# Cross network on one core: transposes and scaled additions interleaved by half-batches, and two neighbouring rows per partition moved by one 4 MB transfer

## The chip, the core and the metric

The kernel runs on one NeuronCore of a Trainium2 chip. The core has a matrix engine (PE, or TensorE), a vector engine (DVE), a scalar engine (ACT), a general engine (POOL), a sequencer that only issues transfers here (SP), and 16 DMA engines that move data between HBM (main memory, "DRAM" in the code) and SBUF (on-chip memory with 128 partitions). The metric is the device time in microseconds of one execution.

## The reference

The input `x0` has 16384 rows of 4096 float32 numbers (256 MiB), and the output has the same shape. Six layers are applied, each with a weight vector and a bias vector of 4096 numbers:

```python
def step(x, wb):
    wi, bi = wb
    xw = jnp.matmul(x, wi)          # one number per row
    x_new = x0 * xw + bi + x
    return (x_new, None)
x, _ = jax.lax.scan(step, inputs, (w, b))
```

After every layer `x` is a multiple of `x0`, one factor per row, plus a vector `c` that is the same for all rows (the sum of the biases so far). So the kernel needs the six dot products of every row of `x0` with the weights, and the constants `cw` (the dot products of `c` with the weights). The factor of a row follows from a recurrence of six steps, factor = factor × (1 + dot) + cw. The output row is factor × x0 + `c_last`.

## The kernel before, in words

The 16384 rows are 128 tiles of 128 rows. A tile is `[128 partitions x 4096]` float32, which is 2 MB (2,097,152 bytes), a row to a partition. Two tiles are a batch (`TB = 2`), so there are 64 batches. SBUF holds eight tiles (`tiles`, slots 0 to 7), which is four batches (`BR = 4`). Slot `s` is loaded for the next time when the store from it has landed.

Every batch goes through these steps:

- SP loads the two tiles, with one transfer each (L141 for the first eight, L145 afterwards). L144 waits for the semaphore `y_stored[s]` of the slot.
- DVE transposes the batch in 32x32 blocks into `blocks`, in four chunks of 128x2048 (L267). Before a chunk it waits until PE is done with that chunk of the batch before (L290).
- PE multiplies the chunks with the weights: 128 matrix products into `dots` (L350).
- ACT copies `dots` four times into `spread` under a mask (L197); PE reduces that to `turned` (L364); ACT adds one and writes `growth` (L202).
- DVE runs the recurrence of six steps, one scan for each tile (L274), and then "finishes" each tile: `tiles = tiles * scale + c_last`, 128x4096, in place (L280).
- ACT stores each finished tile with one transfer (L209).

What sets the order is the program order of each engine, with semaphores between the engines. On DVE it is written in `transpose_and_finish`: four chunks of batch n, then the finish of tile 1 of batch n-1, then the scans of batch n, then the finish of tile 0 of batch n. On ACT the two stores of batch n-1 stand ahead of `make_growth` of batch n, the second of them waiting for the finish of tile 1 of batch n-1. DVE, ACT and SP each run this in a loop over rounds of four batches, with the first round and parts of the last written out.

Ahead of the first batch the weights are loaded into slot 7 four times at different partitions and transposed (L136, L250), and `c_last` is made by PE and ACT (L332, L187). The last batch is finished and stored in eight pieces of 128x1024 (L314, L227), so that the final transfer is small.

The matrix products of a batch start as soon as chunk 0 is transposed, and follow the transposes chunk by chunk.

Of the kernel before, what the change touches and what calls it, by code (L numbers as in the profile page):

```python
# [9 lines left out]
P = 128  # L24
Q = 32
G = P // Q
TB = 2
BR = 4
KM = 2
NCHUNK = 4  # L30
# [4 lines left out]
PIECES = 4  # L35


def cross_network(nc, x, w, b, out):
# [13 lines left out]
    PW = D // PIECES  # L52
    w_rows = w.rearrange("l d a -> l (d a)")
# [3 lines left out]
    with ExitStack() as ctx:  # L57
# [39 lines left out]
        x_landed = [sem(f"x_landed{s}") for s in range(n_slots)]  # L97
        y_stored = [sem(f"y_stored{s}") for s in range(n_slots)]
# [27 lines left out]
        @block.sync  # L126
        def _(sp):
            sp.dma_start(strips_b[:], b_strips).then_inc(strips_b_landed, 16)
            sp.dma_start(strips_w[:], w_strips).then_inc(strips_w_landed, 16)
            sp.dma_start(b_stage, b).then_inc(b_landed, 16)  # L130
            sp.dma_start(tiles[:, 0, :], x[0:P, :]).then_inc(x_landed[0], 16)
# [5 lines left out]
            for s in range(1, n_slots):  # L137
                if s == n_slots - 2:
                    sp.wait_ge(scratch_filled, n_halves)
                    sp.wait_ge(weights_ready, 1)  # L140
                sp.dma_start(tiles[:, s, :], x[s * P:(s + 1) * P, :]).then_inc(x_landed[s], 16)  # L141
# [40 lines left out]
        @block.scalar  # L182
        def _(act):

            for h in range(n_halves):
                act.wait_ge(scratch_filled, h + 1)
                nc.scalar.copy(c_last[:, h * HALF:(h + 1) * HALF], scratch[:]).then_inc(scratch_copied, 1)  # L187
            act.wait_ge(cw_all_ready, 1)
            nc.scalar.copy(cw[:], cw_all[:]).then_inc(cw_ready, 1)

            def make_growth(batch, first=False):
                act.wait_ge(blocks_used, (batch + 1) * NCHUNK)  # L192
                if first:
                    act.wait_ge(group_mask_ready, 1)

                for g in range(G):
                    nc.scalar.activation(spread[:, :, :, g, :], dots[:], ACT.Copy,  # L197
                                         scale=group_mask[:, g:g + 1]).then_inc(dots_spread, 1)
                act.wait_ge(turned_ready, batch + 1)
                if not first:  # L200
# [4 lines left out]
            def store(batch, round_, q):  # L205
                for t in range(TB):
                    s = q * TB + t
                    act.wait_ge(tiles_done, batch * TB + t + 1)
                    act.dma_start(out[bass.ds((round_ * n_slots + s) * P, P), :],  # L209
                                  tiles[:, s, :]).then_inc(y_stored[s], 16)  # L210

            make_growth(0, first=True)
            for q in range(1, BR):
                store(q - 1, 0, q - 1)
                make_growth(q)
            with act.Fori(1, n_rounds) as r:
                store(r * BR - 1, r - 1, BR - 1)
                make_growth(r * BR)
                for q in range(1, BR):
                    store(r * BR + q - 1, r, q - 1)  # L220
                    make_growth(r * BR + q)

            for n in range(TB * PIECES):
                s = n_slots - TB + n // PIECES
                at = slice(n % PIECES * PW, (n % PIECES + 1) * PW)
                act.wait_ge(tiles_done, n_tiles - TB + n + 1)
                act.dma_start(out[(n_tiles - n_slots + s) * P:(n_tiles - n_slots + s + 1) * P, at],  # L227
                              tiles[:, s, at]).then_inc(y_stored[s], 16)
            for s in range(n_slots):
                last_stores = 1 if s < n_slots - TB else PIECES  # L230
                act.wait_ge(y_stored[s], 16 * (n_rounds - 1 + last_stores))

        @block.vector
        def _(dve):
# [3 lines left out]
            def transpose_tile(t):  # L238

                dve.wait_ge(x_landed[t], 16)  # L240
# [25 lines left out]
            def transpose_chunk(batch, q, c):  # L266
                nc.vector.transpose(blocks[:, c, :, :].rearrange("p t n -> p (t n)"),  # L267
                                    tiles[:, q * TB:(q + 1) * TB, c * CH:(c + 1) * CH]
                                    ).then_inc(blocks_ready, 1)

            def scan(batch, q):
                dve.wait_ge(growth_ready, batch + 1)  # L272
                for t in range(TB):
                    nc.vector.tensor_tensor_scan(scale[:, q % 2, t, 0:L], growth[:, t, 0:L], cw[:, 0:L],  # L274
                                                 1.0, ALU.mult, ALU.add).then_inc(scale_ready, 1)

            def finish(batch, q, t):
                s = q * TB + t
                dve.wait_ge(scale_ready, batch * TB + t + 1)  # L279
                nc.vector.scalar_tensor_tensor(out=tiles[:, s, :], in0=tiles[:, s, :],  # L280
                                               scalar=scale[:, q % 2, t, L - 1:L], in1=c_last[:],
                                               op0=ALU.mult, op1=ALU.add).then_inc(tiles_done, 1)

            def transpose_and_finish(batch, q, landed, last=False):

                for s in range(q * TB, (q + 1) * TB):
                    dve.wait_ge(x_landed[s], landed)
                for c in range(NCHUNK):
                    dve.wait_ge(blocks_used, (batch - 1) * NCHUNK + c + 1)  # L289
                    transpose_chunk(batch, q, c)  # L290
                finish(batch - 1, (q - 1) % BR, TB - 1)
                scan(batch, q)
                for t in range(0 if last else TB - 1):
                    finish(batch, q, t)

            dve.wait_ge(scratch_copied, n_halves)
            dve.wait_ge(cw_ready, 1)
            scan(0, 0)
            for t in range(TB - 1):
                finish(0, 0, t)  # L300
            for q in range(1, BR):
                transpose_and_finish(q, q, 16)
            with dve.Fori(1, n_rounds - 1) as r:
                for q in range(BR):
                    transpose_and_finish(r * BR + q, q, r * 16 + 16)
            for q in range(BR):
                transpose_and_finish((n_rounds - 1) * BR + q, q, n_rounds * 16, last=(q == BR - 1))

            dve.wait_ge(scale_ready, n_tiles)
            for n in range(TB * PIECES):  # L310
# [4 lines left out]
                                               scalar=scale[:, (BR - 1) % 2, t, L - 1:L], in1=c_last[:, at],  # L315
# [77 lines left out]
```

## Time and profile before

| | us |
|---|---|
| time, median of 3 runs | 1411.83 |
| lowest and highest run | 1409.92, 1413.0 |
| span of the profiled execution | 1412.7 |
| DVE busy | 1151.1 (81%) |
| PE busy | 694.4 (49%) |
| ACT busy | 95.6 (7%) |
| queue of the loads (q1), share of 16 engines | 49.8% |
| queue of the stores (q10), share of 16 engines | 47.1% |
| data moved | 537.63 MB, mean 381 GB/s |

The span is the time from the first to the last instruction of one execution under the profiler. "Busy" is the time in which an engine worked on an instruction; issuing a transfer and waiting are not counted. The share of a DMA queue is the time that its packets took, over the time of all 16 DMA engines. MB and GB are powers of ten in the profile, so that a "2048 KB" tile is 2.097 MB. The profiled execution is 0.9 us above the median of the three runs and within their spread. Time, span and every duration below are from this kernel alone.

### The profile page before, as it was taken

What the parts mean: (1) busy time and instruction counts of PE and PEld (TensorE: products, weight loads), DVE (VectorE), ACT (ScalarE), POOL (GpSimd) and SP (SyncE); (2) the same over time, 40 slices, a digit from 0 to 9 for tenths busy, and PEclk for the clock granted to TensorE, in tenths of its full rate; (3) what the DMA queues carried; (4) which work ended last, traced back from release to release, by engine and by line L of the source; (5) the groups of instructions that cost most, each with busy time, mean ns of one, the idle gap of its engine ahead of it and who ended that gap; (6) DMA issues with size and microseconds to landing.
All of it is one profiled execution on the core that took longest, in us unless ns stands there. A gap on an engine that the chain in (4) does not pass through costs nothing.

```text
span 1412.7 us, 20472 instructions
## 1 busy us (share of the span) xinstructions
PE 694.4 (49%) x8724; PEld 662.6 (47%) x8724; DVE 1151.1 (81%) x529; ACT 95.6 (7%) x324; POOL 7.2 (1%) x32
## 2 busy tenths in 40 slices
PE   7455455364454553553544544535436445455352
PEld 4445455354454453553544544535435445455352
DVE  4879788878788797787887877878878878779777
ACT  1000000000000000000000000000000000000000
POOL 2000000000000000000000000000000000000000
PEclk9777676777676776766766767667677777677776
DMA  9999999999999999999999999999999999999956
GB/s 318 372 407 387 386 397 394 395 401 388 392 389 383 381 401 394 383 386 391 389 381 394 386 387 383 392 385 387 393 387 391 387 388 386 390 379 393 392 244 263
DMA packets 38016, 537.63 MB, mean 381 GB/s; under 512 B 4254, under 2 KB 4446, under 8 KB 5470
## 3 DMA queue, kind: packets, MB, share of 16 engines
q1 hardware_dynamic: 18716, 269.13, 49.8%
q10 hardware_dynamic: 19296, 268.44, 47.1%
q8 instruction: 2, 0.03, 0.0%
q14 instruction: 2, 0.02, 0.0%
HBM read 269.12 MB, written 268.44 MB: 381 GB/s over the span
## 4 chain that ended last, share of the span: by engine, by line
DVE 61%; issue 20%; PE 7%; ACT 6%; ACTq 2%; DVEq 1%; DMA 1%; SPq 0%
DVE blocks L267 40%; DVE tiles L280 20%; PE turned L364 7%; ACT spread L197 5%; ACTq L209 2%; ACT growth L202 1%; DMA tiles<-in_L_rec_w_dram 1%; DVE scale L274 1%; PE dots L350 1%; DVEq L289 1%; DVE tiles L314 1%; ACTq L201 0%; ACTq L192 0%; DVEq L279 0%; DVEq L272 0%
## 5 line engine op out<-in xcount | busy, mean ns | idle before, releaser
L350 PE MATMUL dots<-blocks,weights 128*64 128x128 f32 x8192 | 585.8, 316 | 466.8 <-DVE blocks L267 466.1
L350 PEld LDWEIGHTS dots<-blocks,weights 128*64 128x64 f32 x8192 | 570.2, 165 | 473.0 <-DVE blocks L267 472.0
L280 DVE SCALAR_TENSOR_TENSOR tiles<-tiles,scale,c_last 128x4096 f32<-128x4096 f32 x126 | 562.5, 4464 | 0.0
L267 DVE STREAM_TRANSPOSE blocks<-tiles 128x2048 f32<-128x2048 f32 x252 | 559.7, 2279 | 0.0
L274 DVE TENSOR_TENSOR_SCAN scale<-growth,cw 128x6 f32<-128x6 f32 x128 | 15.7, 164 | 244.5 <-ACT growth L202 244.5
L364 PE MATMUL turned<-layer_sel,spread 128*128 128x8 f32 x512 | 92.5, 308 | 227.9 <-ACT spread L197 227.9
L364 PEld LDWEIGHTS turned<-layer_sel,spread 128*128 128x128 f32 x512 | 86.6, 255 | 243.3 <-ACT spread L197 243.3
L197 ACT ACTIVATE spread<-dots,group_mask 128x128 f32<-128x128 f32 x256 | 73.0, 368 | 1179.0 <-DVE tiles L280 1168.4
L202 ACT ACTIVATE growth<-turned,ones 128x16 f32<-128x16 f32 x64 | 17.5, 273 | 103.8 <-PE turned L364 103.8
L242 DVE STREAM_TRANSPOSE blocks<-tiles 128x1024 f32<-128x1024 f32 x8 | 9.2, 1210 | 8.8 <-DMA tiles<-in_r_inputs_dram 8.8
L332 PE MATMUL scratch<-tiles,ones 6*128 6x512 f32 x16 | 14.4, 1076 | 2.0 <-ACT c_last L187 2.0
L332 PEld LDWEIGHTS scratch<-tiles,ones 6*128 6x128 f32 x16 | 5.0, 326 | 10.5 <-issue 6.2
L314 DVE SCALAR_TENSOR_TENSOR tiles<-tiles,scale,c_last 128x1024 f32<-128x1024 f32 x8 | 9.7, 1281 | 0.0
L250 DVE STREAM_TRANSPOSE weights<-tiles 128x4096 f32<-128x4096 f32 x1 | 4.4, 4446 | 3.1 <-DMA tiles<-in_L_rec_w_dram 3.1
L187 ACT COPY c_last<-scratch 128x2048 f32<-128x2048 f32 x2 | 3.7, 1865 | 18.5 <-PE scratch L332 18.5
L323 PE MATMUL strips_c<-strips_b,earlier 96*96 96x256 f32 x2 | 1.1, 672 | 5.0 <-POOL earlier L155 5.0
L168 POOL TENSOR_SCALAR_AFFINE_SELECT layer_sel<-layer_sel 128x8 f32<-128x8 f32 x16 | 3.1, 192 | 2.1
L235 DVE MEMSET tiles<- 128x2048 f32 x1 | 1.8, 1765 | 1.3 <-PEq L382 1.3
L323 PEld LDWEIGHTS strips_c<-strips_b,earlier 96*96 96x96 f32 x2 | 0.4, 256 | 5.0 <-issue 5.0
L337 PEld LDWEIGHTS cw_all<-cw_diag,ones 96*128 96x128 f32 x2 | 0.5, 313 | 3.9 <-DVE cw_diag L259 3.9
L149 POOL MEMSET tiles<- 128x2048 f32 x1 | 1.8, 1804 | 0.3 <-POOLq L382 0.3
L337 PE MATMUL cw_all<-cw_diag,ones 96*128 96x8 f32 x2 | 0.6, 372 | 2.3 <-DVE cw_diag L259 2.3
(18 smaller groups left out, 5.3 us busy)
## 6 DMA issues: line engine op xcount, KB each, us to landing
tiles<-in_r_inputs_dram SPq DMA_DIRECT2D x128, 2048.0 KB, 11.3
out_dram<-tiles ACTq DMA_DIRECT2D x126, 2048.0 KB, 9.6
out_dram<-tiles ACTq DMA_DIRECT2D x8, 512.0 KB, 3.1
tiles<-in_L_rec_w_dram SPq DMA_DIRECT2D x4, 96.0 KB
strips_b<-in_L_rec_b_dram SPq DMA_DIRECT2D x1, 96.0 KB, 2.0
strips_w<-in_L_rec_w_dram SPq DMA_DIRECT2D x1, 96.0 KB, 2.0
tiles<-in_L_rec_b_dram SPq DMA_DIRECT2D x1, 96.0 KB
```

The source lines that it names most:

```text
L197: nc.scalar.activation(spread[:, :, :, g, :], dots[:], ACT.Copy, scale=group_mask[:, g:g + 1]).then_inc(dots_spread, 1)
L202: nc.scalar.activation(growth[:], turned[:], ACT.Identity, bias=ones[:, 0:1]).then_inc(growth_ready, 1)
L209: act.dma_start(out[bass.ds((round_ * n_slots + s) * P, P), :], tiles[:, s, :]).then_inc(y_stored[s], 16)
L242: last = nc.vector.transpose(blocks[:, c, t, :], tiles[:, t, c * CH:(c + 1) * CH])
L267: nc.vector.transpose(blocks[:, c, :, :].rearrange("p t n -> p (t n)"), tiles[:, q * TB:(q + 1) * TB, c * CH:(c + 1) * CH]).then_inc(block ...
L274: nc.vector.tensor_tensor_scan(scale[:, q % 2, t, 0:L], growth[:, t, 0:L], cw[:, 0:L], 1.0, ALU.mult, ALU.add).then_inc(scale_ready, 1)
L280: nc.vector.scalar_tensor_tensor(out=tiles[:, s, :], in0=tiles[:, s, :], scalar=scale[:, q % 2, t, L - 1:L], in1=c_last[:], op0=ALU.mult, ...
L289: dve.wait_ge(blocks_used, (batch - 1) * NCHUNK + c + 1)
L314: nc.vector.scalar_tensor_tensor(out=tiles[:, s, at], in0=tiles[:, s, at], scalar=scale[:, (BR - 1) % 2, t, L - 1:L], in1=c_last[:, at], o ...
L332: last = nc.tensor.matmul(scratch[:, c * BANK:(c + 1) * BANK], ones[0:L, :], b_stage[:, at:at + BANK], start=True, stop=True)
L350: last = nc.tensor.matmul(dots[at:at + KM * Q, :, :, :], weights[:, c * KB + k:c * KB + k + KM, :], blocks[:, c, :, k * Q:(k + KM) * Q], s ...
L364: last = nc.tensor.matmul(turned[:, t, :], spread[:, t, m, :, :], layer_sel[:, m, :], start=(m == 0), stop=(m == KM - 1))
```

## The change

The diff has two parts.

**Two rows per partition, one transfer per batch.** A batch is still 256 neighbouring rows of the input. The view `x_pairs` gives partition p the rows 2p and 2p+1 of them, which lie side by side in DRAM (32 KB), and they land side by side in SBUF. One transfer of 4 MB loads a batch and one stores it. There is one semaphore per batch slot (four) where there was one per tile slot (eight). Loads, stores, and the vector work are written out for all 64 batches; only PE keeps its loop.

```diff
+    x_pairs = x.rearrange("(b p t) d -> b p t d", p=P, t=TB)
+    out_pairs = out.rearrange("(b p t) d -> b p t d", p=P, t=TB)
...
-            with sp.Fori(1, n_rounds) as r:
-                for s in range(n_slots):
-                    sp.wait_ge(y_stored[s], r * 16)
-                    sp.dma_start(tiles[:, s, :], x[bass.ds((r * n_slots + s) * P, P), :]).then_inc(x_landed[s], 16)
+            for batch in range(n_pairs, n_batches):
+                j = batch % n_pairs
+                sp.wait_ge(y_stored[j], batch // n_pairs * 16)
+                sp.dma_start(tiles[:, j * TB:(j + 1) * TB, :], x_pairs[batch]).then_inc(x_landed[j], 16)
```

Before the loop SP loads batch 0 as a whole (4 MB) ahead of the weights, and batches 1 to 3 behind them. The first transposes wait for the whole batch 0.

**Half-batches on DVE, and another order on ACT.** DVE now transposes half a batch, scans and finishes one tile of the batch before, transposes the other half, and finishes the other tile. ACT makes `spread` of batch n first, then stores batch n-1 as one transfer once both its tiles are finished, and then makes `growth` of batch n.

```diff
+            for batch in range(1, n_batches):
+                dve.wait_ge(x_landed[batch % n_pairs], (batch // n_pairs + 1) * 16)
+                transpose_chunks(batch, range(0, NCHUNK // 2))
...
+                scan(batch - 1)
+                finish(batch - 1, 0)
+                transpose_chunks(batch, range(NCHUNK // 2, NCHUNK))
+                finish(batch - 1, 1)
+            scan(n_batches - 1)
...
+            for batch in range(1, n_batches):
+                spread_dots(batch)
+                store(batch - 1)
+                make_growth(batch)
```

On DVE in the first batches, the order before was this (L267 transposes of one batch, L280 a finish, L274 the scans):

```order
L280 SCALAR_TENSOR_TENSOR tiles<-tiles,scale,c_last 128x4096
L267 STREAM_TRANSPOSE blocks<-tiles 128x2048 x4
L280 SCALAR_TENSOR_TENSOR tiles<-tiles,scale,c_last 128x4096
L274 SCALAR_TENSOR_TENSOR scale<-growth,cw 128x6 x2
L280 SCALAR_TENSOR_TENSOR tiles<-tiles,scale,c_last 128x4096
```

and now it is this (L254 transposes, L261 the scans, L267 a finish):

```order
L254 STREAM_TRANSPOSE blocks<-tiles 128x2048 x2
L261 SCALAR_TENSOR_TENSOR scale<-growth,cw 128x6 x2
L267 SCALAR_TENSOR_TENSOR tiles<-tiles,scale,c_last 128x4096
L254 STREAM_TRANSPOSE blocks<-tiles 128x2048 x2
L267 SCALAR_TENSOR_TENSOR tiles<-tiles,scale,c_last 128x4096
```

The four transposes of a batch are split two and two. The scans of a batch stood one finish behind its last transpose; now a finish and two transposes of the next batch stand between.

On ACT the order of the early batches before was this (L197 spread, L202 growth, L209 a store of one tile):

```order
L202 ACTIVATE growth<-turned,ones 128x16
L209 DMA out_dram<-tiles 128x4096 x2
L197 ACTIVATE spread<-dots,group_mask 128x4x32 x4
L202 ACTIVATE growth<-turned,ones 128x16
L209 DMA out_dram<-tiles 128x4096 x2
```

and now it is this (L185 spread, L192 growth, L198 a store of a batch):

```order
L192 ACTIVATE growth<-turned,ones 128x16
L185 ACTIVATE spread<-dots,group_mask 128x4x32 x4
L198 DMA out_dram<-tiles 128x8192
L192 ACTIVATE growth<-turned,ones 128x16
L185 ACTIVATE spread<-dots,group_mask 128x4x32 x4
L198 DMA out_dram<-tiles 128x8192
```

The spread of batch n moved ahead of the store of batch n-1, and two stores became one of twice the size.

## Rows read from the trace of the kernel before

**Rows 1.** The page: busy time of each engine, share of the span, instructions.
```profile
PE 694.4 (49%) x8724; PEld 662.6 (47%) x8724; DVE 1151.1 (81%) x529; ACT 95.6 (7%) x324; POOL 7.2 (1%) x32
```
**Rows 2.** The waits: engine, line, released by; total us, times, longest us.
```profile
DVE scale L274 <- ACT growth L202: 244.5, 64, 9.5
```
**Rows 3.** Timeline of two batches on DVE: start us, duration us.
```profile
711.94 8.88 DVE L267 STREAM_TRANSPOSE blocks<-tiles 128x2048 f32<-128x2048 f32 x4
720.74 4.45 DVE L280 SCALAR_TENSOR_TENSOR tiles<-tiles,scale,c_last 128x4096 f32<-128x4096 f32 x1
728.51 0.24 DVE L274 TENSOR_TENSOR_SCAN scale<-growth,cw 128x6 f32<-128x6 f32 x2 [3.33 <-ACT growth L202]
728.72 4.49 DVE L280 SCALAR_TENSOR_TENSOR tiles<-tiles,scale,c_last 128x4096 f32<-128x4096 f32 x1
733.12 8.88 DVE L267 STREAM_TRANSPOSE blocks<-tiles 128x2048 f32<-128x2048 f32 x4
```
**Rows 4.** Timeline of the other engines in the same stretch.
```profile
714.30 8.97 PE L350 MATMUL dots<-blocks,weights 128*64 128x128 f32 x128 [7.40 <-DVE blocks L267]
725.37 0.34 ACTq L209 DMA_DIRECT2D out_dram<-tiles  x1
725.83 1.14 ACT L197 ACTIVATE spread<-dots,group_mask 128x128 f32<-128x128 f32 x4 [18.53 <-DVE tiles L280]
727.02 1.06 PE L364 MATMUL turned<-layer_sel,spread 128*128 128x8 f32 x8 [3.75 <-ACT spread L197]
728.21 0.27 ACT L202 ACTIVATE growth<-turned,ones 128x16 f32<-128x16 f32 x1 [1.24 <-PE turned L364]
```
**Rows 5.** Stretches: us; busy us of each engine; PE clock, DMA share, GB/s.
```profile
0.00:40.00 40.00, 27.10 (x156) 16.64 (x156) 17.30 (x18) 6.59 (x9) 7.24 (x32) 0.98 0.95 329
18.00:46.00 28.00, 16.29 (x146) 12.76 (x146) 16.77 (x14) 3.44 (x7) 0.00 (x0) 0.87 1.00 427
112.00:120.00 8.00, 6.90 (x110) 6.66 (x106) 8.00 (x3) 0.00 (x0) 0.00 (x0) 0.89 1.00 430
200.00:1300.00 1100.00, 539.66 (x6916) 522.45 (x6911) 908.72 (x408) 72.06 (x255) 0.00 (x0) 0.71 0.99 389
718.00:726.00 8.00, 5.27 (x96) 5.03 (x93) 7.19 (x3) 0.17 (x1) 0.00 (x0) 1.00 0.94 393
726.00:729.00 3.00, 1.06 (x8) 0.97 (x8) 0.49 (x3) 1.24 (x5) 0.00 (x0) 0.86 1.07 339
```
**Rows 6.** DMA queues from 112 to 120 us: packets, MB, share of 16 engines.
```profile
q10 hardware_dynamic: 110, 1.80, 52.6%
q1 hardware_dynamic: 101, 1.64, 47.9%
```
**Rows 7.** Loads L145 of the whole run, then stores L209: issue to landing.
```profile
DMA to landing us min/median/max: 9.5/11.2/15.9
DMA to landing us min/median/max: 6.3/9.6/15.3
```
**Rows 8.** The load L145 and the store L209 issued at 107.5 and 107.7.
```profile
L145 SPq DMA_DIRECT2D tiles<-in_r_inputs_dram x1: 333/333/333, 107.5 to 107.5; - x1
L209 ACTq DMA_DIRECT2D out_dram<-tiles x1: 356/356/356, 107.7 to 107.7; - x1
DMA to landing us min/median/max: 14.6/14.6/14.6
```
**Rows 9.** The last load L145, and its landing.
```profile
L145 SPq DMA_DIRECT2D tiles<-in_r_inputs_dram x1: 333/333/333, 1341.6 to 1341.6; - x1
DMA to landing us min/median/max: 10.1/10.1/10.1
```
**Rows 10.** Timeline of the start and the end.
```profile
11.97 4.62 DVE L242 STREAM_TRANSPOSE blocks<-tiles 128x1024 f32<-128x1024 f32 x4 [8.76 <-DMA tiles<-in_r_inputs_dram]
19.70 4.45 DVE L250 STREAM_TRANSPOSE weights<-tiles 128x4096 f32<-128x4096 f32 x1 [3.10 <-DMA tiles<-in_L_rec_w_dram]
38.84 0.24 DVE L274 TENSOR_TENSOR_SCAN scale<-growth,cw 128x6 f32<-128x6 f32 x2 [9.49 <-ACT growth L202]
43.56 13.51 ACTq L209 DMA_DIRECT2D out_dram<-tiles  x2
1398.89 0.24 DVE L274 TENSOR_TENSOR_SCAN scale<-growth,cw 128x6 f32<-128x6 f32 x2 [3.86 <-ACT growth L202]
```
**Rows 11.** The two loads L141 issued from 24.2 us: issue to landing.
```profile
DMA to landing us min/median/max: 25.5/29.6/33.6
```
**Rows 12.** The page: DMA packets of the whole execution.
```profile
DMA packets 38016, 537.63 MB, mean 381 GB/s; under 512 B 4254, under 2 KB 4446, under 8 KB 5470
```

More of the change, by code:

```diff
@@ L95, in cross_network @@
         cw_all = ps("cw_all", [P, LP])
-        x_landed = [sem(f"x_landed{s}") for s in range(n_slots)]
-        y_stored = [sem(f"y_stored{s}") for s in range(n_slots)]
+        x_landed = [sem(f"x_landed{s}") for s in range(n_pairs)]
+        y_stored = [sem(f"y_stored{s}") for s in range(n_pairs)]
         w_landed = [sem(f"w_landed{g}") for g in range(G)]
@@ L130, in _ @@
             sp.dma_start(b_stage, b).then_inc(b_landed, 16)
[L131 removed]
+            sp.dma_start(tiles[:, 0:TB, :], x_pairs[0]).then_inc(x_landed[0], 16)
             sp.wait_ge(stage_zeroed, 2)
@@ L198, in make_growth @@
                                          scale=group_mask[:, g:g + 1]).then_inc(dots_spread, 1)
+            def make_growth(batch):
                 act.wait_ge(turned_ready, batch + 1)
-                if not first:
+                if batch > 0:
                     act.wait_ge(scale_ready, batch * TB)
@@ L203, in make_growth, with store @@
                                      bias=ones[:, 0:1]).then_inc(growth_ready, 1)
[L205 to L221, printed above, removed]
+            def store(batch):
+                j = batch % n_pairs
+                act.wait_ge(tiles_done, (batch + 1) * TB)
+                act.dma_start(out_pairs[batch], tiles[:, j * TB:(j + 1) * TB, :]).then_inc(y_stored[j], 16)
+            spread_dots(0)
+            make_growth(0)
+            for batch in range(1, n_batches):
+                spread_dots(batch)
+                store(batch - 1)
+                make_growth(batch)
             for n in range(TB * PIECES):
@@ L226, in _ @@
                 act.wait_ge(tiles_done, n_tiles - TB + n + 1)
[L227 to L231, printed above, removed]
+                act.dma_start(out_pairs[n_batches - 1, :, n // PIECES, at],
+                              tiles[:, s, at]).then_inc(y_stored[n_pairs - 1], 16)
+            for j in range(n_pairs):
+                last_stores = 1 if j < n_pairs - 1 else TB * PIECES
+                act.wait_ge(y_stored[j], 16 * (n_batches // n_pairs - 1 + last_stores))
         @block.vector
@@ L264, in _, with transpose_chunks @@
                 transpose_tile(t)
[L266 to L271, printed above, removed]
+            def transpose_chunks(batch, chunks):
+                at = batch * TB % n_slots
+                for c in chunks:
+                    dve.wait_ge(blocks_used, (batch - 1) * NCHUNK + c + 1)
+                    nc.vector.transpose(blocks[:, c, :, :].rearrange("p t n -> p (t n)"),
+                                        tiles[:, at:at + TB, c * CH:(c + 1) * CH]
+                                        ).then_inc(blocks_ready, 1)
@@ L279, in finish @@
                 dve.wait_ge(scale_ready, batch * TB + t + 1)
                 nc.vector.scalar_tensor_tensor(out=tiles[:, s, :], in0=tiles[:, s, :],
-                                               scalar=scale[:, q % 2, t, L - 1:L], in1=c_last[:],
+                                               scalar=scale[:, batch % 2, t, L - 1:L], in1=c_last[:],
                                                op0=ALU.mult, op1=ALU.add).then_inc(tiles_done, 1)
[L284 to L307, printed above, removed]
+            for batch in range(1, n_batches):
+                dve.wait_ge(x_landed[batch % n_pairs], (batch // n_pairs + 1) * 16)
+                transpose_chunks(batch, range(0, NCHUNK // 2))
+                if batch == 1:
+                    dve.wait_ge(scratch_copied, n_halves)
+                    dve.wait_ge(cw_ready, 1)
+                scan(batch - 1)
+                finish(batch - 1, 0)
+                transpose_chunks(batch, range(NCHUNK // 2, NCHUNK))
+                finish(batch - 1, 1)
```

22 lines of the change are left out of this document (12 added, 10 removed).

## The prediction

> **What bounds the kernel now.** I read the busy times first, then the waits, the timeline of two batches, the stretches with their DMA columns, and the landings. The shares alone mislead here. DVE is busy for 81% of the span [rows 1], and the DMA engines for 99% of the steady stretch [rows 5], and either could pass for the limit.
>
> The waits decide it. DVE has no wait for a load in the steady part. Its one large wait is the scan's for `growth`: 244.5 us in 64 times [rows 2], and without the first (9.5 us) 3.73 us each. From the scan at 38.84 to the one at 1398.89 [rows 10] there are 63 periods of 21.59 us. In one of them [rows 3] DVE transposes (8.8 us from start to next start), finishes a tile (4.4), waits, scans (0.2) and finishes another (4.4), about 17.9 us of work and 3.7 of wait. The reader is to see that nothing is left over: DVE's chain, work plus this wait, is the period. The last load lands at 1341.6 + 10.1 = 1351.7 [rows 9], 61 us before the end, so landed tiles pile up ahead of DVE. That is the sign that DVE is the bound and the transfers are not.
>
> The transfers are close behind. In 28 us with loads alone the rate is 427 GB/s; in 8 us with a load and a store side by side, both queues sharing the engines about evenly [rows 6], it is 430; over the 1100 steady us it is 389 [rows 5]. A batch moves 2 x 4.194 = 8.389 MB, which is 19.5 us at 430 and 21.57 at 389. So the engines are occupied throughout, but 2.07 us of every batch go to slow places. Two of them show in rows 5: from 718 to 726, with a gap between two stores, 393 GB/s; from 726 to 729, with a load just about to take over from a store, 339.
>
> **The wait on DVE.** The wait is a chain that starts when the finish ends at 725.2: the store's issue (0.34) and its surroundings, `spread` at 725.83 (1.14), `turned` at 727.02 (1.06), `growth` at 728.21 (0.27), scan at 728.51 [rows 3, 4]. `dots` had been ready since 714.30 + 8.97 = 723.27, 2.45 us after the last transpose. In the new order the scan of batch n comes after a finish (4.4) and two transposes (4.5) have followed the last transpose, 8.9 us of cover. In that time PE needs 2.45, `spread` 1.2, `turned` 1.1 to 1.9 and `growth` 0.3, about 5.9. Only `growth` may stand behind the store, which is issued at 4.4 + 0.3 and takes 0.34, so it is ready at about 5.5 to 6. The whole wait goes: 3.7 us a batch, and DVE needs 17.9 to 18.1. If PE's last chunk took twice its 2.45 us at a lower clock, the chain would be 8.4 and still covered. If the cover were gone the old wait would be back.
>
> What is late next is the transfer. DVE would allow 64 x 18.1 = 1158 us, while 537.63 MB [rows 12] at 430 GB/s are 1250.3. So of 3.7 us a batch at most 21.59 - 19.5 = 2.1 can be had.
>
> **One transfer of 4 MB where there were two.** ACT and SP issue 63 and 64 transfers fewer, at 0.34 us, on sequencers that nobody waits for: nothing. The rate of a 32 KB run has no row. Between loads alone (427) and mixed (430) I see no sign that runs of 16 KB lose anything, so I take 430. Its effect is on the loop. The slot is now a whole batch, and there are four. Store n-1 is issued only after both finishes, which come after the load of batch n has landed and 18.1 us of DVE. Load n+3 waits for that store. This circle spans three periods: DVE 18.1, two issues 0.4, the store S and the load L from issue to landing. The shortest store took 6.3 us for 2.1 MB [rows 7], 4.9 of data at 430 and 1.4 more. Fully shared, half of the rate each, a 4 MB transfer takes 19.5 + 1.4 = 20.9. That gives (18.5 + 41.8) / 3 = 20.1 us a period as the lower bound for a circle that always shares. The upper bound is from the one pair that was issued together: load and store both took 14.6 [rows 8], 9.75 of shared data and 4.85 of other delay. With 19.5 of shared data they take 24.35 each, and the period is (18.5 + 48.7) / 3 = 22.4. I take the middle, 21.2. It is above the 19.5 of pure data and below the 21.57 that the present mixture of slow places would give.
>
> The Trainium skill (DMA: Bandwidth & Descriptors, "Queues, rings and completion order") says that a DMA engine goes round robin between the queues that have work. By that rule load and store share whenever both are out, as in the circle above. Rows 6 agree, with shares of 52.6% and 47.9%. The Trainium skill (HBM Reference, "Specifications (TRN2)") gives about 358 GB/s for each core of a pair and about 425 for a core that streams alone. By the first number this kernel's data alone would take an estimated 1502 us, and the trace is below that already at 389 GB/s, so the measurement decides against it. By the second the data would take an estimated 1265 us instead of 1250, and the sum would be 15 us higher.
>
> **Start.** The first 40 us moved 329 GB/s [rows 5], against 430 a loss of 40 x (1 - 329/430) = 9.4 us; the weights cause it and stay. Batch 0 lands 4.9 us later than at 11.97. The weights queue behind it: transposed from 24.6 to 29.1, the second tile of batch 0 until 34.4. The dot products of batch 0 took 10.0 us in the trace and end at about 41, the scan is possible at 43.8, and with a finish, two transposes and a finish (4.4 + 4.5 + 4.4) store 0 is issued at 57.3 instead of 43.56 [rows 10]. The initial loads end earlier: the last of eight landed at about 24.6 + 33.6 = 58.2 [rows 11] with a 4.9 us store ahead of it, so its data would end at about 52. Idle DMA: 58.3 - 52 = 6 us, which counts now that DMA is the bound.
>
> **End.** When the last load lands, store 61 has been out for 21.2 - 18.3 = 2.9 us and ends 8 us later. Store 62 is issued 18.3 us after the landing. About 12.4 us of the DMA engines are empty, and the last landing adds 1.4: 13.8. The last batch's pieces queue behind store 62 and are data.
>
> **Sum.** 1250.3 + 9.4 + 6 + 13.8 + 60 periods x (21.2 - 19.5) = 102, together 1381.5 us for the span. The profiled execution lies 0.9 above the median, so the forecast is 1380 us.
>
> **The rivals.**
> A. The slow places stay as they are, 2.07 us a batch: 1279.5 + 124 = 1404, less 0.9: 1403. For it: a queue still starts afresh beside the other twice a batch at most, as now. Against it: the gap between the two stores of a batch goes, and more of the time is shared, as at 112 to 120 us, with no loss.
> B. Load and store share nearly always and the losses vanish: 19.8 us a period, 1279.5 + 18 = 1297. For it are the 430 GB/s of rows 5; against it the circle, whose lower bound is 20.1.
> C. Slower: the circle through the 4 MB buffers becomes the bound. The place is the wait for `y_stored` ahead of a load and the wait for `x_landed` ahead of the transposes. The price is that of the pair of rows 8: 22.4 a period, 1279.5 + 60 x 2.9 = 1453. It decides from the point where L + S exceeds 3 x 21.72 - 18.5 = 46.7 us, since 1412.7 = 1279.5 + 60 x 2.22. For it: the longest landings of 2 MB are 15.9 and 15.3 [rows 7], and four large slots smooth less than eight small ones. Against it: the medians, doubled, give 22.4 + 19.2 = 41.6.
> D. The change does not do what it says: `growth` is late again behind the store on ACT, or PE falls behind with two chunks at a time, and DVE's period is 21.6 as before. Then 1412, no change. The 2.9 us of spare cover speak against it.
>
> **How the numbers follow.** The forecast holds 48% (1345 to 1397 as its own range), A 17%, B 11%, C 17%, D 7%. Within 0.2% (2.8 us), about what a measurement of this kernel can tell from no change, is D. Faster: 48 + 17 + 11 = 76%. Slower: C, 17%. The range: the bounds 20.1 and 22.4 of the period give 1315 to 1453; I cut half of B at the low end and half of C at the high end, 1325 to 1428.
>
> **What would show it.** Right: DVE's wait for `growth` is below 20 us in total, and a wait for the loads of 2.5 to 3.5 us a batch has taken its place; the rate from 200 to 1300 us is between 391 and 403 GB/s; loads and stores land after 19 to 23 us; the last load lands about 42 us before the end. Wrong: a rate at or under 386 GB/s with L + S over 47 us (C), a rate over 410 (B), or scans that still wait for ACT (D). If the DMA share of the steady stretch falls clearly below 0.97, the circle starves the engines, whatever the sum.

## The result and the profile after

The changed kernel takes 1332.51 us (median of 4 runs, 1329.51 to 1334.39) against 1411.81 us (4 runs) before: a ratio of 0.9437, 95% interval 0.9422 to 0.9452. That is 79 us less. The direction of the forecast was right and the time lies in its range, but the forecast of 1380 promised 32 of these 79 us, and the time is below the 1345 to 1397 of its main case. The profiled execution of the changed kernel took 1329.51 us, its span is 1327.6. In the experiments a median is of all runs of a kernel, while a ratio and its interval leave out any run that is over 1.5% above the fastest of the same kernel (one run in each of two kernels).

The first part of the page, and the waits (waiting engine and line, releaser, us in total, times, longest):

```profile
PE 776.4 (58%) x8724; PEld 725.4 (55%) x8724; DVE 1151.0 (87%) x529; ACT 95.9 (7%) x324; POOL 7.3 (1%) x32
```

```profile
DVE blocks L254 <- DMA tiles<-in_r_inputs_dram: 143.1, 59, 6.5
...
DVE scale L261 <- ACT growth L192: 4.7, 2, 3.9
```

DVE did the same work (1151.0 us, against 1151.1 in [rows 1]). Its 244.5 us of waiting for `growth` [rows 2] are 4.7 now, in two waits. In their place stand 143.1 us of waiting for loads, 2.4 us in each of 59 batches. Before, that line did not exist: the bound has moved from DVE to the transfers. The timeline of one batch on DVE and ACT shows how the chain is hidden (start us, duration us):

```profile
702.00 0.20 DVE L261 TENSOR_TENSOR_SCAN scale<-growth,cw 128x6 f32<-128x6 f32 x2
702.17 4.49 DVE L267 SCALAR_TENSOR_TENSOR tiles<-tiles,scale,c_last 128x4096 f32<-128x4096 f32 x1
706.57 4.50 DVE L254 STREAM_TRANSPOSE blocks<-tiles 128x2048 f32<-128x2048 f32 x2
...
710.99 4.44 DVE L267 SCALAR_TENSOR_TENSOR tiles<-tiles,scale,c_last 128x4096 f32<-128x4096 f32 x1
...
713.13 1.15 ACT L185 ACTIVATE spread<-dots,group_mask 128x128 f32<-128x128 f32 x4 [16.05 <-PE dots L324]
...
715.46 0.34 ACTq L198 DMA_DIRECT2D out_dram<-tiles  x1
715.90 0.27 ACT L192 ACTIVATE growth<-turned,ones 128x16 f32<-128x16 f32 x1 [1.62 <-DVE tiles L267]
716.43 4.51 DVE L254 STREAM_TRANSPOSE blocks<-tiles 128x2048 f32<-128x2048 f32 x2 [1.00 <-DMA tiles<-in_r_inputs_dram]
...
720.86 0.20 DVE L261 TENSOR_TENSOR_SCAN scale<-growth,cw 128x6 f32<-128x6 f32 x2
```

`growth` is ready at 716.17, and the scan that needs it starts at 720.86, 4.7 us later. DVE's wait of 1.00 us for a load lies in between, so 3.7 us would be left without it. The stretches (us; busy us of PE, weight loads, DVE, ACT, POOL; PE clock, DMA share, GB/s):

```profile
0.00:40.00 40.00, 25.54 (x148) 15.15 (x148) 20.69 (x17) 5.82 (x7) 7.27 (x32) 1.00 0.95 346
40.00:60.00 20.00, 14.43 (x168) 13.91 (x170) 17.94 (x10) 2.20 (x8) 0.00 (x0) 0.79 0.61 261
200.00:1200.00 1000.00, 588.19 (x6696) 556.07 (x6694) 881.23 (x395) 69.48 (x245) 0.00 (x0) 0.77 1.00 414
```

The steady rate is 414 GB/s, against 389 in [rows 5], and 8.389 MB at 414 are 20.26 us a batch. The DMA share was 0.99 and is 1.00: the engines were hardly less occupied before, and moved 6% less. So the share of a DMA queue does not say how fast its packets go. Nor does the 389 show what the transfers could do: DVE took a batch every 21.59 us, and 8.389 MB in 21.59 us are 389 GB/s. The landings, of the loads L134 and then of the stores L198, both of 4 MB:

```profile
DMA to landing us min/median/max: 15.6/22.4/24.6
DMA to landing us min/median/max: 11.2/20.3/24.3
```

### The profile page after: what moved, and what is told of

Same layout as the page of the kernel before. It is cut to its first block, busy times and chain, and to the rows that moved or that the text cites. A ratio compares the mean times of both kernels' runs of the same rounds, so it can differ in the third digit from the quotient of the medians.

```text
span 1327.6 us, 19167 instructions
## 1 busy us (share of the span) xinstructions
PE 776.4 (58%) x8724; PEld 725.4 (55%) x8724; DVE 1151.0 (87%) x529; ACT 95.9 (7%) x324; POOL 7.3 (1%) x32
## 4 chain that ended last, share of the span: by engine, by line
DMA 66%; DVE 21%; PE 6%; issue 5%; ACT 1%; DVEq 0%; SPq 0%; ACTq 0%
DMA tiles<-in_r_inputs_dram 33%; DMA out_dram<-tiles 31%; DVE blocks L254 13%; DVE tiles L267 6%; PE dots L324 6%; DMA tiles<-in_L_rec_w_dram 1%; ACT spread L185 1%; DVE tiles L288 1%; DVE scale L261 0%; DVE tiles L219 0%; DVEq L46 0%; DVE blocks L226 0%; PE turned L338 0%; SPq L125 0%; ACT growth L192 0%
## 5 line engine op out<-in xcount | busy, mean ns | idle before, releaser
L324 PE MATMUL dots<-blocks,weights 128*64 128x128 f32 x8192 | 692.8, 348 | 436.5 <-DVE blocks L254 435.7
L324 PEld LDWEIGHTS dots<-blocks,weights 128*64 128x64 f32 x8192 | 657.6, 184 | 461.8 <-DVE blocks L254 460.7
L254 DVE STREAM_TRANSPOSE blocks<-tiles 128x2048 f32<-128x2048 f32 x252 | 567.2, 2289 | 143.7 <-DMA tiles<-in_r_inputs_dram 143.1
L267 DVE SCALAR_TENSOR_TENSOR tiles<-tiles,scale,c_last 128x4096 f32<-128x4096 f32 x126 | 562.5, 4464 | 0.0
L185 ACT ACTIVATE spread<-dots,group_mask 128x128 f32<-128x128 f32 x256 | 73.2, 369 | 1104.7 <-PE dots L324 1104.7
L338 PE MATMUL turned<-layer_sel,spread 128*128 128x8 f32 x512 | 67.7, 259 | 79.6 <-ACT spread L185 79.6
L338 PEld LDWEIGHTS turned<-layer_sel,spread 128*128 128x128 f32 x512 | 61.9, 191 | 95.1 <-ACT spread L185 95.1
L192 ACT ACTIVATE growth<-turned,ones 128x16 f32<-128x16 f32 x64 | 17.6, 274 | 81.6 <-PE turned L338 54.0
L261 DVE TENSOR_TENSOR_SCAN scale<-growth,cw 128x6 f32<-128x6 f32 x128 | 13.1, 142 | 4.7 <-ACT growth L192 4.7
L176 ACT COPY c_last<-scratch 128x2048 f32<-128x2048 f32 x2 | 3.7, 1866 | 18.5 <-PE scratch L306 18.5
## 6 DMA issues: line engine op xcount, KB each, us to landing
tiles<-in_r_inputs_dram SPq DMA_DIRECT2D x64, 4096.0 KB, 22.5
out_dram<-tiles ACTq DMA_DIRECT2D x63, 4096.0 KB, 20.3
```

Source lines behind the costliest of these rows:

```text
L192: nc.scalar.activation(growth[:], turned[:], ACT.Identity, bias=ones[:, 0:1]).then_inc(growth_ready, 1)
L261: nc.vector.tensor_tensor_scan(scale[:, batch % 2, t, 0:L], growth[:, t, 0:L], cw[:, 0:L], 1.0, ALU.mult, ALU.add).then_inc(scale_ready, 1)
L324: last = nc.tensor.matmul(dots[at:at + KM * Q, :, :, :], weights[:, c * KB + k:c * KB + k + KM, :], blocks[:, c, :, k * Q:(k + KM) * Q], s ...
L338: last = nc.tensor.matmul(turned[:, t, :], spread[:, t, m, :, :], layer_sel[:, m, :], start=(m == 0), stop=(m == KM - 1))
```

## The experiments

Every ratio is to the kernel before, timed on the same chip. The two theories at the start were these. Theory 1: removing DVE's wait gives the whole gain, since it keeps both queues supplied. Theory 2: the 4 MB transfers with 32 KB runs raised the rate.

**Two 2 MB transfers in the place of each 4 MB one.** The new order stays.

```diff
-                j = batch % n_pairs
                 act.wait_ge(tiles_done, (batch + 1) * TB)
-                act.dma_start(out_pairs[batch], tiles[:, j * TB:(j + 1) * TB, :]).then_inc(y_stored[j], 16)
+                for t in range(TB):
+                    s = (batch * TB + t) % n_slots
+                    act.dma_start(out[(batch * TB + t) * P:(batch * TB + t + 1) * P, :],
+                                  tiles[:, s, :]).then_inc(y_stored[s], 16)
```
(and the loads likewise)

> The new order of the vector and scalar engines as in the changed kernel, but each 4 MB transfer replaced by two of 2 MB issued at the same point, one row per partition (16 KB runs). Theory 1 (the gain is the removed wait on DVE, and the transfers only had to be kept out all the time): about the time of the changed kernel, 1325 to 1345 us, steady rate 410 to 417 GB/s. Theory 2 (the large transfers with 32 KB runs are what raised the rate): DMA-bound at the old 389 GB/s, 1395 to 1410 us.

Measured: 1329.27 us, ratio 0.9414 (0.9398 to 0.943), steady rate 415 GB/s. With transfers of the size and layout of the kernel before, the whole gain is there. Theory 2 falls. This kernel has the new order and also the written-out loops; the run with the old order below tells how much the second can be worth.

**4 MB transfers with 16 KB runs.**

```diff
-    x_pairs = x.rearrange("(b p t) d -> b p t d", p=P, t=TB)
-    out_pairs = out.rearrange("(b p t) d -> b p t d", p=P, t=TB)
+    x_pairs = x.rearrange("(b t p) d -> b p t d", p=P, t=TB)
+    out_pairs = out.rearrange("(b t p) d -> b p t d", p=P, t=TB)
```

> The changed kernel with 4 MB transfers that give partition p the rows p and p+128 of a batch, so each run in DRAM is 16 KB. Theory 1: no difference to the changed kernel within 0.5% (1326 to 1339 us). Theory 2, in the form that the length of a run matters: slower, 1370 us or more, with packets of 611 ns and slow ones as before; in the form that the size of a transfer matters: as the changed kernel.

Measured: 1325.83 us, ratio 0.9391 (0.937 to 0.9412). The 32 KB runs gain nothing. This version is even 0.5% ahead of the changed kernel, with intervals of the ratio that do not overlap.

**The old order with 4 MB transfers.**

```diff
+            scan(0)
+            finish(0, 0)
             for batch in range(1, n_batches):
...
+                transpose_chunks(batch, range(0, NCHUNK))
                 finish(batch - 1, 1)
-            scan(n_batches - 1)
+                scan(batch)
+                if batch < n_batches - 1:
+                    finish(batch, 0)
...
+                store(batch - 1)
                 spread_dots(batch)
-                store(batch - 1)
                 make_growth(batch)
```

> 4 MB transfers with 32 KB runs, but the old order: four transposes, finish of tile 1, scan, finish of tile 0 on DVE, and the store ahead of spread on ACT. Theory 1: DVE waits 3.7 us a batch for growth again and is the bound, period 21.6, 1410 to 1425 us (the start costs some us more than before). Theory 2: part of the gain stays, 1350 to 1390.

Measured: 1393.29 us, ratio 0.9869 (0.9852 to 0.9885), lower than theory 1 said and not in theory 2's span either. Two waits of this kernel, and three rows of its timeline:

```profile
DVE scale L261 <- ACT growth L192: 215.0, 64, 8.1
ACT growth L192 <- PE turned L338: 89.9, 64, 2.0
```

```profile
710.28 4.44 DVE L267 SCALAR_TENSOR_TENSOR tiles<-tiles,scale,c_last 128x4096 f32<-128x4096 f32 x1
714.75 0.34 ACTq L198 DMA_DIRECT2D out_dram<-tiles  x1
...
715.14 1.14 ACT L185 ACTIVATE spread<-dots,group_mask 128x128 f32<-128x128 f32 x4 [18.31 <-DVE tiles L267]
```

The second wait in the kernel before:

```profile
ACT growth L202 <- PE turned L364: 103.8, 64, 2.1
```

DVE waits for `growth` as in [rows 2], and not for loads, so it is the bound again. But the wait is shorter: (215.0 - 8.1) / 63 = 3.28 us a batch against 3.73. Of these 0.45 us, 0.15 lie between the end of the finish and the store's issue (0.03 here, 725.37 - 725.19 = 0.18 in [rows 3, 4]) and 0.07 between the store's issue and `spread` (0.39 against 0.46): ACT has no loop registers to work on here. Another 0.22 a batch are in the wait for `turned` (89.9 against 103.8 in total); why it is shorter is not shown. The scans run from 41.3 to 1373.3, a period of 21.14 us against 21.59: 0.45 x 63 = 28 us, of which some 2.5 are lost again at the start (first scan at 41.3, not 38.84) and some 4 at the end, where 18.0 us follow the last scan and not 13.8. So the written-out loops and the 4 MB transfers together bring about 19 us with the old order, and going on to the new order brings the other 61. The orders on DVE and on ACT were changed back together, so what each of them is worth was not separated.

**4 MB loads, each tile stored after its own finish.**

```diff
+                store(batch - 1, 0)
                 spread_dots(batch)
-                store(batch - 1)
+                store(batch - 1, 1)
                 make_growth(batch)
```

> The changed kernel with 4 MB loads, but every tile stored by its own 2 MB transfer right after its own finish, the first of them 9 us earlier than now. If the circle through the 4 MB buffers (load, vector work, store, load) sets the period of 20.2 us: it shortens, the wait of DVE for loads stays or falls, 1310 to 1328 us. If the DMA engines' own losses set it: steady rate unchanged at 412 to 417 GB/s, and only start and end gain, up to 8 us: 1322 to 1335; more, shorter transfers with more starts could even cost 10 to 20 us.

Measured: 1376.01 us, ratio 0.9743 (0.9715 to 0.977), 44 us slower than the changed kernel and far from both expectations' middle. The steady rate was 395 GB/s. Three explanations stood: the separate stores cost starts, or it was their meeting with the loads of 4 MB and 32 KB packets, or the layout of their rows.

**The same with 2 MB loads and 16 KB runs on both sides** (the kernel with two 2 MB transfers, and the edit above on ACT).

> The kernel with the new order and two 2 MB transfers per batch each way (row per partition, 16 KB runs), which took 1329 us; here the first tile of a batch is stored right after its own finish, 9 us before the second. Theory 'starts' (every transfer that starts on an empty queue beside the other queue costs the DMA engines about a microsecond, and single stores start more often): 1365 to 1385 us, steady rate 393 to 400 GB/s, as the run with single stores and 4 MB loads (1376). Theory 'mixed packets' (that run was slow because 16 KB packets of the stores shared the engines with 32 KB packets of the loads, or because every second row was left out in DRAM): no loss here, 1320 to 1335.

Measured: 1303.98 us, ratio 0.9175 (0.9157 to 0.9193). The six runs form two groups, three from 1294.67 to 1296.71 and three from 1311.25 to 1316.33; the median lies between them, where no run is, and the ratio stands for about 1295 us. Against two 2 MB stores issued together (1329.27), separate stores gain 2.5% in the first group and about 1% in the second. Theory "starts" fails as stated. In the window from 200 to 1200 us of the profiled execution (1313.65, in the second group) the rate in 40 slices is:

```profile
GB/s 431 431 431 430 429 423 426 422 423 410 418 412 416 402 419 422 414 405 411 417 416 414 406 425 409 420 416 419 428 409 419 424 418 420 401 410 415 414 411 407
```

The kernel runs at 430 to 431 for the first 100 us of this window and then loses 3% without any change in its program. So its order and its sizes alone do not fix the rate; what does was not tested.

**The same transfers, with every second row in each.** The edit is shown against the kernel of 1303.98 us. Partition p again holds rows 2p and 2p+1, and each 2 MB transfer takes one of them.

```diff
-                    sp.dma_start(tiles[:, s, :], x[(batch * TB + t) * P:(batch * TB + t + 1) * P, :])
+                    sp.dma_start(tiles[:, s, :], x_pairs[batch, :, t, :])
```
(and the stores likewise)

> As the run with two 2 MB transfers each way and a store after each finish (1304 us), but partition p holds the neighbouring rows 2p and 2p+1, so each 2 MB transfer takes every second row of the batch in DRAM, in 16 KB runs, on both queues. Theory 'mixed packets' (the run with 4 MB loads and single stores, 1376 us, was slow because the loads' 32 KB packets alternate with the stores' 16 KB packets, which gives a store a third of the rate and makes it land late): no mixture here, 1295 to 1318. Theory 'every second row': 1355 to 1390.

Measured: 1294.52 us, ratio 0.917 (0.9153 to 0.9187); three runs took 1294.25 to 1294.66 and one 1320.7. Leaving out every second row costs nothing. The profiled execution (1294.38) also starts fast and slows down, less than the one of 1313.65. The stretches of the latter, then of this one:

```profile
200.00:400.00 200.00, 123.09 (x1387) 116.62 (x1385) 180.27 (x82) 14.13 (x50) 0.00 (x0) 0.77 1.01 428
800.00:1200.00 400.00, 239.63 (x2682) 227.91 (x2684) 353.35 (x161) 28.27 (x100) 0.00 (x0) 0.75 1.00 415
```

```profile
200.00:400.00 200.00, 124.42 (x1386) 118.16 (x1386) 180.77 (x82) 14.14 (x50) 0.00 (x0) 0.76 1.01 428
800.00:1200.00 400.00, 237.19 (x2725) 223.85 (x2726) 359.59 (x162) 28.54 (x101) 0.00 (x0) 0.78 1.01 423
```

What remains for the 1376 us are the loads, and they differ in two things: 4 MB in one transfer, and packets of 32 KB. No run has single stores beside 4 MB loads of 16 KB packets, so the two are not separated. The landings of the stores in the run of 1376, then of the loads and stores in the run of 1303.98 (the page's list of issues: KB each, median us):

```profile
out_dram<-tiles ACTq DMA_DIRECT2D x126, 2048.0 KB, 20.0
```

```profile
tiles<-in_r_inputs_dram SPq DMA_DIRECT2D x128, 2048.0 KB, 20.4
out_dram<-tiles ACTq DMA_DIRECT2D x126, 2048.0 KB, 15.4
```

A 2 MB store takes 20.0 us beside the 4 MB loads and 15.4 beside 2 MB loads. The theory "mixed packets" explained this by a turn: if the engines took packets of both queues alternately, a store with 16 KB packets would get a third of the rate beside 32 KB packets. The Trainium skill (DMA: Bandwidth & Descriptors, "Queues, rings and completion order") says that a DMA engine goes round between its queues packet by packet. The changed kernel's trace agrees from 658 to 674 us, where load and store move the same number of packets (queue: packets, MB, share of 16 engines):

```profile
q1 hardware_dynamic: 104, 3.41, 49.6%
q10 hardware_dynamic: 104, 3.41, 49.4%
```

The run of 1376 us does not show such turns in the stretch that was looked at. Stores were issued at 622.1 and 630.9 us and the next load at 635.1. From 627 to 637 us, and then from 637 to 648:

```profile
q10 hardware_dynamic: 265, 4.08, 96.7%
q1 hardware_dynamic: 19, 0.10, 2.4%
```

```profile
q1 hardware_dynamic: 124, 4.06, 102.6%
q10 hardware_dynamic: 23, 0.11, 2.5%
```

The stores have the engines nearly to themselves, then the load has them. By 637 us the stores' queue had moved 4.08 MB, nearly all of its two stores (4.19 MB), and yet the store of 630.9 landed only at 656.3, after 25.4 us; while the load ran, 0.11 MB of store data trickled through. So here a store is late because little remains of it for long, and not because it gets a third of the rate throughout. Why that little remains, and whether the landing waits for it, is open. Packets of the two sizes were not tried the other way round (large in the stores).

**Less vector work.** Each finish covers half of the columns; the other half of the output rows stays unscaled, except in the last batch.

```diff
-                nc.vector.scalar_tensor_tensor(out=tiles[:, s, :], in0=tiles[:, s, :],
-                                               scalar=scale[:, batch % 2, t, L - 1:L], in1=c_last[:],
+                nc.vector.scalar_tensor_tensor(out=tiles[:, s, 0:D // 2], in0=tiles[:, s, 0:D // 2],
+                                               scalar=scale[:, batch % 2, t, L - 1:L], in1=c_last[:, 0:D // 2],
```

> The changed kernel with each finish cut to half of the columns (the other half of every output row is the input, unscaled, except in the last batch); DVE's work per batch falls from 18.1 to 13.7 us. If the circle load, DVE, store, load sets the period: (13.7 + 0.4 + 42.8) / 3 = 19.0, so the transfers alone bound it at 19.5 to 19.8: 1285 to 1312 us, steady rate 424 to 430. If the DMA engines' own losses set it: unchanged rate of 412 to 418, 1315 to 1332 (a few us less at start and end).

Measured: 1301.86 us, ratio 0.9227 (0.9205 to 0.9248), steady rate 420 GB/s, so 19.97 us a batch. The time is in the circle's span, the rate lies between the two expectations.

```profile
DVE blocks L254 <- DMA tiles<-in_r_inputs_dram: 383.8, 60, 13.6
```

```profile
tiles<-in_r_inputs_dram SPq DMA_DIRECT2D x64, 4096.0 KB, 23.3
out_dram<-tiles ACTq DMA_DIRECT2D x63, 4096.0 KB, 23.1
```

DVE gives 4.4 us a batch and waits 6.4 for loads. Of the 4.4 us, spread over three periods 1.5, only 0.29 reach the period. The rest turned into longer waits of DVE and longer landings, 46.4 us for load and store together against 42.8. So DVE's part of the circle has little to give in the changed kernel: when it gets shorter, the landings stretch.

**Three slots instead of four.**

```diff
-    n_pairs = n_slots // TB
+    n_pairs = n_slots // TB - 1
```
(and slot numbers modulo three)

> The changed kernel with three batch slots of 4 MB in SBUF instead of four. The circle now spans two periods: (18.5 + L + S) / 2, where L and S fall to 11.2 each if they never share the engines. Circle theory: not below (18.5 + 22.3) / 2 = 20.4, and with starts that cost a microsecond 21 to 23: 1375 to 1500 us, steady rate 365 to 400 GB/s, DMA share clearly below 1. If slots did not matter and only the DMA engines' losses did: as now, 1325 to 1340.

Measured: 1470.17 us, ratio 1.0423 (1.0404 to 1.0443), steady rate 373 GB/s, DMA share 0.91.

```profile
200.00:1200.00 1000.00, 537.43 (x6055) 510.23 (x6055) 794.63 (x356) 63.52 (x224) 0.00 (x0) 0.74 0.91 373
```

```profile
tiles<-in_r_inputs_dram SPq DMA_DIRECT2D x64, 4096.0 KB, 13.2
out_dram<-tiles ACTq DMA_DIRECT2D x63, 4096.0 KB, 14.3
```

The circle is real. Here it binds: (18.5 + 13.2 + 14.3) / 2 = 23.0 by the medians, 22.5 by the rate, and the engines stand idle for 9%. With four slots the same sum gives (18.5 + 22.5 + 20.3) / 3 = 20.4, and the rate 20.26.

**Transfers alone.** PE, ACT and DVE do nothing for the batches; a tile (2 MB) or a batch (4 MB) is stored when it has landed.

> Transfers alone: the preamble stays, but PE, ACT and DVE do nothing for the batches, and each tile of 2 MB (16 KB runs) is stored when it has landed, so the output is the input. Both queues always have work. If a queue that never runs empty costs nothing: 427 to 432 GB/s from 200 to 1200 us, 1265 to 1280 us. If mixing reads and writes itself costs: at or under 417.

> The same with 4 MB transfers of 32 KB runs, a batch stored when it has landed. If the size of transfer and run matter for the rate at all, it shows here, by 1% or more against the 2 MB copy; otherwise both are equal within 0.5%, 1265 to 1285 us.

Measured: 1261.36 us (ratio 0.8935, 0.8917 to 0.8954) and 1261.55 us (0.8937, 0.8917 to 0.8957). The two kernels' stretches:

```profile
200.00:1200.00 1000.00, 0.00 (x0) 0.00 (x0) 0.00 (x0) 0.00 (x0) 0.00 (x0) 1.00 1.01 431
```

```profile
200.00:1200.00 1000.00, 0.00 (x0) 0.00 (x0) 0.00 (x0) 0.00 (x0) 0.00 (x0) 1.00 1.00 433
```

A load lands after 31.5 or 38.5 us here, and a store after 40.2 or 39.2, so both queues always have work. Then mixing loads and stores costs nothing: 19.4 us a batch, at either size. No run moved these bytes in less time, so 1261 us is the mark to measure a version by.

**Two versions meant to be faster.** The first is the kernel with 2 MB transfers, with tile 0 loaded ahead of the weights, and single stores only in batches 0 and 62.

> A version meant to be the fastest: new order, two 2 MB transfers per batch (16 KB runs) as in the run that took 1329 us; in addition tile 0 is loaded ahead of the weights and tile 1 behind them, and only in batch 0 and batch 62 the first tile is stored right after its own finish. Steady part unchanged (415 GB/s). The start gains up to 5 us and the end up to 9 us of idle DMA time: 1314 to 1325. If start and end were not on the path: 1327 to 1331.

Measured: 1318.24 us, ratio 0.9338 (0.9323 to 0.9352). 11 us less than the kernel with 2 MB transfers, at the same steady rate of 415 GB/s: they come from start and end, the only places that the edit touches. The second has single stores throughout, and loads each tile as soon as its own store has landed:

```diff
                 for t in range(TB):
                     sp.wait_ge(y_stored[j * TB + t], batch // n_pairs * 16)
-                load(batch)
+                    load(batch, [t])
```

> A version meant to be the fastest: the run that took 1304 us (new order, 2 MB transfers of 16 KB runs, each tile stored after its own finish), with tile 0 loaded ahead of the weights and each tile loaded again as soon as its own store has landed, without waiting for the other tile of the batch. The circle becomes shorter for the first tile of a batch, and the start gains up to 5 us: 1283 to 1300. If more separate starts cost the DMA engines more than the shorter circle gives: 1305 to 1340.

Measured: 1286.07 us (5 runs, 1285.83 to 1291.13), ratio 0.9119 (0.9103 to 0.9135), the fastest of all and 46 us under the changed kernel.

```profile
0.00:60.00 60.00, 42.31 (x356) 30.82 (x356) 43.18 (x29) 8.01 (x14) 7.24 (x32) 0.94 0.97 370
200.00:1200.00 1000.00, 598.09 (x6864) 565.13 (x6864) 902.05 (x406) 70.69 (x250) 0.00 (x0) 0.78 1.01 425
```

425 GB/s are 19.74 us a batch, and the first 60 us move 370 GB/s.

## Why the prediction was right and wrong, point by point

**The bound before** was read rightly: DVE's chain with its wait. The old order brings the wait back, and with it the bound (1393 us); the new order with transfers of the old size has the whole gain (1329).

**The removed wait** was right. It is down to 4.7 us in total. `growth` was ready 5.1 us after the last transpose in the batch shown (5.5 to 6 forecast).

**What is late next** was right in kind. The transfers are, with 2.4 us of wait for a load per batch (just under the 2.5 to 3.5 forecast), and median landings of 22.4 and 20.3 us (19 to 23). The rate missed its sign: 414 GB/s, where 391 to 403 was to confirm the forecast and over 410 was to show rival B.

**The size and the runs of the transfers** were put at no gain, and this held in three comparisons: 2 MB against 4 MB, 16 KB against 32 KB runs, and the two copies.

**The period is the step that failed.** The forecast took 21.2 us, the middle of 20.1 and 22.4. Measured are 20.26 at 414 GB/s. The term was 60 x (21.2 - 19.5) = 102 us; it is 60 x (20.26 - 19.5) = 46. This one term is 56 us too long and accounts for the error of the span: 1381.5 - 56 = 1325.5, measured 1327.6.

What was mis-sized in it is the sum L + S of the landings. Between 41.8 us at the lower and 48.7 at the upper bound the forecast took the middle, 45.2, without a reason; the medians add up to 42.8. The upper bound was read from the pair of [rows 8], 14.6 us each, and all that went beyond the shared data was counted as delay that every transfer has. But the load L145 ahead of it was issued at 100.7:

```profile
L145 SPq DMA_DIRECT2D tiles<-in_r_inputs_dram x1: 333/333/333, 100.7 to 100.7; - x1
...
DMA to landing us min/median/max: 12.2/12.2/12.2
```

It landed at 112.9, 5.4 us after the load of [rows 8] was issued. From 107.5 to 111.5 us the queue of the stores (q10) moved nothing at all, and the queue of the loads (q1) was full, mostly with the load ahead:

```profile
q1 hardware_dynamic: 97, 1.43, 104.4%
q14 instruction: 1, 0.01, 0.5%
```

So 4 to 5 of the 14.6 us were a wait for the load ahead, and the store had it too, though it was in another queue. In the changed kernel such pairs exist, but they are not the rule: the load of 653.8 and the store of 654.5 us landed after 24.0 and 23.5 us, near the 24.35 of the upper bound, and the store of 675.5 after 18.2, below the 20.9 of the lower. With nothing at all for the line the forecast would be 1250.3 + 29.2 + 60 x 0.6 = 1316, which is too low.

The mechanism behind the term was right only in part. The circle of DVE work, store and load is there, and it binds with three slots. With four it adds up as well, (18.5 + 42.8) / 3 = 20.4, but that does not make it the cause: the run with less vector work took 4.4 us out of it, which should have shortened the period until the pure data set it, and got 0.29 us, because the landings grew. The forecast computed the period from the landings; here the landings stretched when the circle got shorter, and the period hardly moved.

The last step from span to time was also off, by about 3 us. In every run of the two kernels with both numbers the time is 1.8 to 1.9 us above its span. The forecast took 0.9 off, from a span of 1412.7 us beside a median of times of 1411.83.

**Start and end.** The first 60 us moved 19.1 MB, where 430 GB/s would be 25.8: 15.6 us lost against 15.4 forecast (9.4 + 6). The sum is partly luck: the first 40 us lost 7.8 (346 GB/s) and the next 20 lost 7.9 (261 GB/s). Store 0 was issued at 55.7 (57.3 forecast). The last load landed 1327.6 - 1287.8 = 39.8 us before the end (42 forecast):

```profile
L134 SPq DMA_DIRECT2D tiles<-in_r_inputs_dram x1: 327/327/327, 1264.5 to 1264.5; - x1
...
DMA to landing us min/median/max: 23.3/23.3/23.3
```

**The rivals.** A (the slow places stay, 1403) fell: what stands above 19.5 went from 2.07 us a batch to 20.26 - 19.5 = 0.8. The 2.07 were never shown to be a price of the transfers, since DVE asked for no more than 389 GB/s. B (no losses, 19.8 us a period, 1297 us) was nearer than the forecast of 21.2 and 1380, and the sign for it came true, but 0.8 us a batch of loss stayed. It is what the copies do, and what the fastest version comes near with 19.74. C is the run with three slots, at 1470: right as a mechanism, and absent with four. D did not come about.

**What stays open.** Why the changed kernel stays 0.8 us a batch above pure data is not shown. In the three runs with 4 MB transfers in which these and not DVE or the slots set the pace, the loss falls as landings get longer: 0.8 us with L + S of 42.8, 0.5 with 46.4 (less vector work), none with 77.7 (copy, 4 MB). Slow places such as 726 to 729 us in [rows 5] lie where one queue takes over from the other. That each take-over costs is not shown: single stores, which start more often, were faster beside 2 MB loads and slower beside 4 MB loads.

## What to carry to other kernels

When two resources both look full, look at which one lets finished work pile up ahead of it, take that one's wait away, and price what is left by a copy of the same bytes (here 1261 us). A landing time taken from a loaded trace contains the line ahead of it, in its own queue and here also in the other one: look at what was issued before it, and use the median of many landings and not one pair. A loop of landings adds up to the period whatever the cause, so shorten one part of it in a run before calling it the bound. And when buffers go round in a circle, freeing and refilling them in smaller pieces can help, as it did here with 2 MB on both queues (1286 us); with 4 MB loads beside 2 MB stores it cost 44 us.

## What was not expected of the hardware

- Loads of 4 MB in 32 KB packets beside single stores of 2 MB in 16 KB packets cost 6% (ratio 0.9743 against 0.9175 for the same stores with 2 MB loads of 16 KB packets), while both sides large or both sides small made no difference (1332.51, 1329.27). Whether the packet or the transfer size does it is open.
- A transfer can wait for one in the other queue: the store of 107.7 us moved nothing until 111.5, while the load ahead of it used the engines.
- One program can change its transfer rate while it runs: 430 to 431 GB/s for 100 us and 417 over the 1000 us. Its runs fall into two groups, near 1295 and above 1311 us.
- Loads and stores side by side reach the rate of loads alone, 431 to 433 GB/s in the copies and 427 in [rows 5].
